# Nine-operation inverse square roots, and the second key copy of each batch on ScalarE, in a four-layer attention and feed-forward kernel

## The reference

```python
x = x + jnp.tanh(g_xattn[0]) * _L0_xattn_ref(_layernorm(x), ctx_512, ...)      # layer-normed scores, softmax
x = x + jnp.tanh(g_ffn[0])   * _L0_ffn_ref(_layernorm(x), ...)                 # 64 routed experts, 4 chosen, 2 shared
x = x + jnp.tanh(g_xattn[1]) * _L1_xattn_ref(_layernorm(x), ctx_512, ctx_512)  # 32 query heads, 8 key heads of 8
x = x + jnp.tanh(g_ffn[1])   * _L1_ffn_ref(_layernorm(x), ...)                 # rms norms, causal attention, gated FFN
x = x + jnp.tanh(g_xattn[2]) * _L2_xattn_ref(ctx_512, _layernorm(x), ...)      # sigmoid of a sum of two projections
x = x + jnp.tanh(g_ffn[2])   * _L2_ffn_ref(_layernorm(x), ...)                 # rms/layer norms, quantised products
x = x + jnp.tanh(g_xattn[3]) * _L3_xattn_ref(_layernorm(x), ctx_512, ctx_512, ...)
x = x + jnp.tanh(g_ffn[3])   * _L3_ffn_ref(_layernorm(x), ...)                 # soft mixture of 16 experts
```

```python
def _layernorm(x, axis=-1, eps=1e-05):
    m = jnp.mean(x, axis=axis, keepdims=True)
    v = jnp.var(x, axis=axis, keepdims=True)
    return (x - m) / jnp.sqrt(v + eps)
```

## Time and profile before

| | us |
|---|---|
| Median of 3 executions | 1252.83 (1251.37 to 1256.25) |
| The profiled execution | 1256.97 |
| Its span | 1255.2 |
| TensorE busy | 1052.1 (84%) |
| VectorE busy | 745.6 (59%) |
| ScalarE busy | 524.0 (42%) |
| GpSimd busy | 327.9 (26%) |

### The profile page before, as it was taken

How to read it: one execution, slowest core, us unless ns; L and a number is a source line. 1 busy time by engine, 2 the same in 40 slices (tenths; PEclk the granted TensorE clock), 3 DMA queues, 4 the chain that set the end, 5 groups by cost and what they waited for, 6 DMA issues and landing times.

```text
span 1255.2 us, 18970 instructions
## 1 busy us (share of the span) xinstructions
PE 1052.1 (84%) x6625; PEld 668.9 (53%) x6625; DVE 745.6 (59%) x1684; ACT 524.0 (42%) x882; POOL 327.9 (26%) x626
## 2 busy tenths in 40 slices
PE   4459999999999788877988899991463878999997
PEld 2248888888887443332456535550322534566575
DVE  6775454444546558677565311579697674684644
ACT  1222333333333467555544530233473553544533
POOL 7023343433436336324343200001310300000000
PEclk9999999999999779889999999896696789999999
DMA  6201211112350000000000300002000000000000
GB/s 149 44 1 28 48 43 45 47 41 50 107 150 28 1 2 3 2 3 2 3 3 4 119 1 1 1 1 51 1 2 1 3 2 1 1 9 1 9 9 10
DMA packets 62444, 32.09 MB, mean 26 GB/s; under 512 B 47104, under 2 KB 61072, under 8 KB 62112
## 3 DMA queue, kind: packets, MB, share of 16 engines
q1 hardware_dynamic: 62368, 31.10, 9.4%
HBM read 29.64 MB, written 1.05 MB: 24 GB/s over the span
## 4 chain that ended last, share of the span: by engine, by line
PE 70%; DVE 20%; issue 3%; ACT 3%; POOL 1%; DMA 1%; SPq 0%; DVEq 0%; POOLq 0%; ACTq 0%; PEldq 0%
PE bank L771 16%; PE bank L787 8%; PE bank L884 4%; PE bank L1173 3%; PE bank L1102 2%; PE bank L999 2%; PE bank L1357 2%; DVE mx L2298 2%; PE bank L967 2%; PE bank L1374 2%; PE bank L929 2%; PE bank L1359 2%; PE bank L1153 2%; PE bank L1206 1%; DVE mxc L2298 1%
## 5 line engine op out<-in xcount | busy, mean ns | idle before, releaser
L2298 DVE TENSOR_REDUCE mx<-bank 128x2 f32<-128x512 f32 (+1 forms) x176 | 119.0, 690 | 84.9 <-PE bank L1102 48.3
L1731 ACT ACTIVATE prob<-bank 128x512 f32<-128x512 f32 x176 | 102.8, 597 | 95.4 <-PE bank L1153 68.0
L1536 ACT ACTIVATE hhi<-hh 128x512 fp32r<-128x512 f32 x72 | 45.5, 632 | 153.2 <-DVE hh L2134 140.4
L2130 DVE TENSOR_TENSOR hu<-bank,sg 128x512 f32<-128x512 f32 x64 | 44.3, 692 | 96.5 <-PE bank L771 96.5
L771 PE MATMUL bank<-xh,wh 128*128 128x512 f32 x288 | 91.4, 398 | 0.0
L771 PE MATMUL bank<-xh,wl 128*128 128x512 f32 x288 | 90.1, 393 | 0.0
L771 PE MATMUL bank<-xlo,wh 128*128 128x512 f32 x288 | 90.0, 394 | 0.0
L2122 DVE TENSOR_TENSOR hlo<-hh,hhi 128x512 fp32r<-128x512 f32 x72 | 57.4, 797 | 50.3 <-ACT hhi L1536 50.3
L2734 POOL TENSOR_TENSOR wl<-wraw,wh 128x512 fp32r<-128x512 f32 x72 | 81.8, 1136 | 13.0 <-POOL wh L2731 13.0
L1601 ACT ACTIVATE sg<-bank 128x512 f32<-128x512 f32 x72 | 43.0, 597 | 59.4 <-PE bank L771 59.3
L771 PEld LDWEIGHTS bank<-xlo,wh 128*128 128x128 f32 x288 | 54.3, 189 | 13.4
(11 more groups left out here) (454 smaller groups left out, 2286.3 us busy)
## 6 DMA issues: line engine op xcount, KB each, us to landing
wraw<-in_L_ffn_wg_dram SPq DMA_DIRECT2D x64, 64.0 KB, 2.3
wraw<-in_L_ffn_wu_dram SPq DMA_DIRECT2D x64, 64.0 KB, 2.3
wraw<-in_L_ffn_wd_dram SPq DMA_DIRECT2D x32, 128.0 KB, 2.4
l_raw<-in_L_ffn_w_dram SPq DMA_DIRECT2D x2, 1024.0 KB, 6.9
mun<-in_L_ffn_mu_dram SPq DMA_DIRECT2D x1, 2048.0 KB, 7.7
xs<-in_x_dram SPq DMA_DIRECT2D x1, 1024.0 KB, 5.5
w1s<-in_L_ffn_W_dram SPq DMA_DIRECT2D x2, 512.0 KB, 8.0
stage<-in_L_ffn_W_in_base_dram SPq DMA_DIRECT2D x1, 1024.0 KB, 8.3
```

Source lines behind the costliest of these rows:

```text
L1536: return act.activation(dst, src, ACT.Copy, scale=scale)
L1731: act.activation(t.prob[k][:, :], bank[3 + n % 2][:, :], ACT.Exp).then_inc(S("probs"), 1)
L2130: tt(hu[k % 2][:, :], bank[4 + (n + 1) % 4][:, :], sg[k % 2][:, :], ALU.mult).then_inc(once("up_used"), 1)
L2298: V.reduce_max(out_, bank[n % 3][:, :].rearrange("p (h t) -> p h t", h=heads), AX, negate=True)\
```

## The change

The inverse root gets two unequal turns instead of three equal ones. The seed has another constant. `rsqrt_first` is a turn with other coefficients (3 operations), and `rsqrt_second` a turn of higher order (4 operations): 9 in all with the seed, in all 26 places. In `between`, n = 2 is the first turn, n = 3 the second, and n = 4 is empty; n = 5 to 7 stay at their steps.

The second copy of a batch's turned keys in the first stream, `("k", s, 1)` of `l1x`, goes from VectorE to a new ScalarE function `keys`, at the same step (slot three ahead, `k` = 7), behind the `exps` of that step. The first copy stays on VectorE. The unused helper `stats` goes. Nothing changes in the programs of TensorE, GpSimd and SyncE but line numbers: behind the new function, lines are higher by 7 to 13 than before.

```diff
+                def keys(s):
+
+                    L, b, g = groups[s]
+                    if b >= 2:
+                        act.wait_ge(S("scores"), tiles_before(stream, LAST[L, b - 2] + 1))
+                    leaves(("k", s, 1), kTx[:, b % 2, 4:8, :], lambda full, half: half[:, :].rearrange("p (h n) -> p h n", h=4))
...
                             if k == 7 and groups[s][0] == "l1f":
                                 queries(s, 1)
+                            if k == 7 and groups[s][0] == "l1x" and groups[s][2] == 0:
+                                keys(s)
...
-                step(ts(out_.bitcast(I32), w.bitcast(I32), -1, 0x5F3759DF, ALU.mult, ALU.add))
-
-            def rsqrt_turn(step, out_, v):
+                step(ts(out_.bitcast(I32), w.bitcast(I32), -1, 0x5F1FFFF9, ALU.mult, ALU.add))
+
+            def rsqrt_first(step, out_, v):
 
                 k = v.shape[1]
                 w = nw[:, 0:k] if k <= 4 else cmr[:, 0:k]
                 step(tt(w, out_, v, ALU.mult))
-                step(stt(out=w, in0=w, scalar=-0.5, in1=out_, op0=ALU.mult, op1=ALU.mult))
-                step(stt(out=out_, in0=w, scalar=1.5, in1=out_, op0=ALU.add, op1=ALU.mult))
+                step(stt(out=w, in0=w, scalar=-0.703952253 * 0.375, in1=out_, op0=ALU.mult, op1=ALU.mult))
+                step(stt(out=out_, in0=w, scalar=0.703952253 * 2.38924456 * 0.375, in1=out_, op0=ALU.add, op1=ALU.mult))
+
+            def rsqrt_second(step, out_, v):
+
+                k = v.shape[1]
+                w = nw[:, 0:k] if k <= 4 else cmr[:, 0:k]
+                step(tt(w, out_, v, ALU.mult))
+                step(stt(out=w, in0=w, scalar=0.375 ** -2, in1=out_, op0=ALU.mult, op1=ALU.mult))
+                step(stt(out=w, in0=w, scalar=-10.0 / 3.0, in1=w, op0=ALU.add, op1=ALU.mult))
+                step(stt(out=out_, in0=w, scalar=5.0, in1=out_, op0=ALU.add, op1=ALU.mult))
 
             def rsqrt(step, out_, v):
 
                 rsqrt_seed(step, out_, v)
-                for _ in range(3):
-                    rsqrt_turn(step, out_, v)
...
-                    elif n < 5:
-                        rsqrt_turn(step, rs[:, 0:4], ve[:, 0:4])
+                    elif n == 2:
+                        rsqrt_first(step, rs[:, 0:4], ve[:, 0:4])
+                    elif n == 3:
+                        rsqrt_second(step, rs[:, 0:4], ve[:, 0:4])
+                    elif n == 4:
+                        pass
...
-                            if k == k1 and ("k", s, 1) in there:
+                            if k == k1 and ("k", s, 1) in there and groups[s][0] != "l1x":
                                 operands(s, ("k", s, 1))
```

More of the change, by code:

```diff
@@ L1971, in rsqrt_turn @@
                 step(tt(w, out_, v, ALU.mult))
-                step(stt(out=w, in0=w, scalar=-0.5, in1=out_, op0=ALU.mult, op1=ALU.mult))
-                step(stt(out=out_, in0=w, scalar=1.5, in1=out_, op0=ALU.add, op1=ALU.mult))
+                step(stt(out=w, in0=w, scalar=-0.703952253 * 0.375, in1=out_, op0=ALU.mult, op1=ALU.mult))
[7 more added lines that the diff above has]
+                step(stt(out=out_, in0=w, scalar=5.0, in1=out_, op0=ALU.add, op1=ALU.mult))
             def rsqrt(step, out_, v):
                 rsqrt_seed(step, out_, v)
-                for _ in range(3):
-                    rsqrt_turn(step, out_, v)
-            def stats(step, src, *scales, between=None, tiles=NT):
-                step(*[V.bn_stats(bn[:, i, :], src(i)) for i in range(tiles)])
-                step(*[V.bn_aggr(mv[:, i, :], bn[:, i, :]) for i in range(tiles)])
-                step(*[ts(ve[:, tiles * k:tiles * k + tiles], mv[:, 0:tiles, 1], m, a, ALU.mult, ALU.add)
-                       for k, (m, a) in enumerate(scales)], *(between() if between else []))
-                rsqrt(step, rs[:, 0:tiles * len(scales)], ve[:, 0:tiles * len(scales)])
+                rsqrt_first(step, out_, v)
+                rsqrt_second(step, out_, v)
             def x_rows(i):
```

## The result

| | before | after |
|---|---|---|
| Median of 4 executions, us | 1252.1 (1249.4 to 1256.3) | 1235.7 (1235.5 to 1239.1) |
| Ratio | | 0.9884 (95%: 0.9851 to 0.9916) |
| In 8 more executions of the same changed kernel, beside 17 of before | 1250.8 (1242.1 to 1257.2) | 1238.8 (1236.1 to 1247.8), ratio 0.9897 (0.9863 to 0.9931) |
| Span of the first profile | 1255.2 | 1233.9 |

The changed kernel is 1.2% faster, some 13 us (16 in the first four executions), where 9.6 us were forecast. The first sample lies outside the range; the median of all twelve, 1238.5, on its edge. Between the two first profiles the difference is even 21.3 us. So 4 to 12 us more than the sum are to be explained.

The account below looks back on a forecast made before the run. TensorE was taken as the main bound, 70% of the chain, with VectorE 20%. Roots 6.3, first root 1.0, batches 2 and 3 2.5, batch 0 -0.25 sum to 9.6 us: median 1243.2, range 1238.5 to 1248.5.

Parts of the forecast that it names:

- Two operations, 0.395 us a place: Inverse roots: two fewer dependent VectorE operations save 0.395 us per place, the new operation form costing the same 0.198.
- Sixteen places on the chain, 6.3 us: Sixteen root places from 51.22 to 1031.02 us lie on the chain and save 0.395 each, 6.3 us.
- The first root, 1.0: Very first root, at 15.5 us: the last `xn` starts ahead of a GpSimd split, saving 1.0 us, up to 1.5.
- Batches 2 and 3, 2.5: Key hand-overs before L1102 at 504.92 and 550.81 us: ScalarE's copy removes TensorE's waits of 1.27 us, 2.5 us together.
- Batch 1, nothing: Key hand-over before 475.38 us: TensorE continues earlier, but GpSimd's key split sets the chain; 0, at most 0.8 us.
- Batch 0, -0.25: Key hand-over at 427.44 us: VectorE has nothing else to do, so ScalarE's slower copy loses 0.25 us.
- Rivals A and D: Only roots show, stream bound elsewhere (6.0 us); or new operation costs two links or a turn stays hidden (6.4). Chance 0.24.
- Rival C: Shifted TensorE idle moments make another long low-clock stretch in the first stream, costing 10 to 14 us; chance 0.06.
- rival B: Shorter waits keep the 10.2 us stretch from 550.00 us at full clock, 4 us more, median 1239.3; chance 0.15.

Follow-up runs that it names:

- before_again: The kernel before, unchanged, run again for a second profile: span 1251.8 us.
- after_again: The changed kernel, unchanged, run again in more executions: median 1238.8 us, profile span 1244.6.
- thirteen: The kernel before with two more small VectorE operations in each of 22 root calls, the four among the stream's maxima unchanged: 1258.4 us, ratio 1.0055.
- _held: The kernel before and the changed one, with unread matmuls in nearly all TensorE waits from 6 to 82 and 401 to 428 us: 1238.9 and 1226.6 us.
- all_but_first: The changed kernel with the eleven-operation root back in the very first place: 1240.1 us, ratio to before 0.9883.
- keys_only: The kernel before with only the second key copy moved to ScalarE, eleven-operation roots kept: 1253.5 us, ratio 0.9987.
- before_warm: The kernel before with 33 unread matmuls on TensorE in five waits between 401 and 428 us: 1247.9 us, ratio 0.9978.
- before_start_busy: The kernel before with unread matmuls in TensorE's waits from 6 to 20 us: 1248.5 us.

## Why the prediction was wrong, point by point

- **Two operations, 0.395 us a place:** right. 2.18 became 1.79; the new form costs a link like the others.
- **Sixteen places on the chain, 6.3 us:** right in the start (0.8 for two of its places together and 0.4 for the third, between `before_again` and `after_again`) and about right over all, as `thirteen` shows (6.6 for 5.1). In the last part, from 792 us on, the places gave 3.2 of 3.2 between the first two profiles, but 1.9 and 1.2 in the pairs `_again` and `_held`; TensorE had 7, 8 and 12 us more of its work at the low level there in the changed kernel, so the level can have eaten the rest. Why it had more isn't shown.
- **The first root, 1.0:** right, 1.18 between the first profiles (1.4 in TensorE's first L704 from `all_but_first` to the changed kernel), and by the mechanism named: the last `xn` got ahead of the split. Two readings behind it were off. The 4.05 us in the earlier trace rows aren't behind a split of the same length but end with GpSimd's two long selects (L2675, 11.08 to 19.52). And the last `xn` was only 0.95 of the 1.65 us that the group was longer than a free one; the first two took 0.82 and 0.69 instead of 0.41. The Trainium skill, page "SBUF — State Buffer", section "Who interferes with whom", was read as leaving only 0.4 or 1.5; its lock is per instruction, and the trace lies between, as two of the four `xn` were still held (0.81 and 0.69; 2.08 us for the four against 1.38 in the earlier trace rows).
- **Batches 2 and 3, 2.5:** right, 1.27 and 1.01. **Batch 1, nothing:** right. **Batch 0, -0.25:** -0.33.
- **Rivals A and D** are out: the waits of 1.27 us are gone or 0.26, and a root saves 0.39. **Rival C** is out too: no new long stretch at the low level came in the stream.
- **The clock** is where it failed, in two terms. *The start:* the sum has no term for TensorE's level there, so nothing, and gives no reason. Its windows showed a granted clock of 1.00 up to 92.6 us that is no measurement; that eight transposes (L704) took 1.97 us there and sixteen of the same shape (L826) 1.94 us at 410.96 was in the trace before, and I had not compared. The early stretch gave 2.5 us (`keys_only`) to 5.1 us (the changed kernel), and was in no rival. *The stretch at 550:* rival B had it, at 4 us and with a chance of 0.15, outside the sum, which kept the clock as it was. In all eight profiles of both edits the stretch is gone, and the stage from 544 to 600 us is 7.0 us shorter or more, for the 1.7 forecast there; but 5.2 of this came in `before_again` without an edit. B's median, 1239.3, is close to the 1238.5 measured. That is partly luck: B left out the start, and its mechanism, the shorter waits at batches 2 and 3, isn't what the runs show, since the stretch is gone with the wait of 1.27 still there.
- **The base:** I set the sum against one profile and a median of three executions. 78 executions of that kernel reach from 1242.1 to 1257.5 us. The range of 10 us that I gave is narrower than the spread of the unchanged kernel alone.
- **The sum itself**, 9.6, lies among what is found where like is compared with like, and is settled by none of it: 7.2 us (profiles with the same start), 8.8 and 14.9 (groups of the same mean clock), 12.0 (busy from 401 us on), 12.3, uncertain between 8 and 17 (start held too). Stage by stage, what goes beyond it lies where TensorE's level differs between the two profiles. That the clock's share comes from the edits as a rule isn't shown.

## What to carry to other kernels

Before a profile's time is used as a base, compare the length of the same TensorE instruction in several stages: it tells at which of its two levels the engine ran, where the record of the clock doesn't. Where two executions of one kernel differ by more than the change is worth, take a second profile of the unchanged kernel first, and compare executions with the same stretches. And an idle TensorE isn't free: what it waits now, it may pay in the next work at half clock. Matmuls that nobody reads, in the waits, gave as much on the kernel before (12 us) as the whole change.

## What was not expected of the hardware

- By their mean clock (0.926 and more), TensorE's start ran at the 1.2 GHz level for up to 92 us in 29 of 78 executions of the same program, and with a stretch of about 10 us at 2.4 GHz near 30 us in the others. With TensorE busy from 6.4 us on, the full level came at 9.2 to 10.6 us in eight profiles of eight.
- It fell during single waits: of 6.26 us at 20 to 26 us, and of 18 us at 40 us. At 550 us it fell in a wait of 1.27 us in four profiles, and in `before_again` it didn't, in the same wait.
- The stretch of 34.1 us at 423.7 us, with 31.35 us of TensorE's work in it, is there in all profiles of kernels with nothing added in TensorE's waits (in one with matmuls added only in the start it was missing), and in none of the eight with matmuls in the five waits ahead of it.
- TensorE's rise by one level doesn't always shorten a stage: the 9.5 us won before 470 in `before_warm` were followed by 2.6 lost up to 544, and in `before_start_busy` the level fell during the wait of 6.26 us that the faster start had made longer.
